# Box layout by VectorE block transposes and four channel picks per image, instead of small matmuls, in a four-layer convolution kernel on one Trainium2 core

## What is computed

```python
h = jnp.einsum('oc,bchw->bohw', w1, x)          # 64 -> 16 channels
h = jax.nn.relu(_bn_train(h, g1, b1))
h = _box_conv(h, x_min, x_max, y_min, y_max)    # 16 -> 64: four boxes for each channel
h = _bn_train(h, g2, b2)
return jax.nn.relu(x + h)
```

## Time and profile before

| what | value |
|---|---|
| runs | 166.64, 165.84, 166.61 us (median 166.61) |
| profiled execution | 165.47 us, of which the span in the trace is 163.7 us |
| PE busy | 147.1 us, 90% |
| DVE, ACT, POOL busy | 110.9, 89.7, 56.9 us |
| L3, by the trace | from about 135 us to 163.7 us |
| granted PE clock, mean | 0.982 of full speed |

### The profile page before, as it was taken

How to read it: one execution, slowest core, us unless ns; L and a number is a source line. 1 busy time by engine, 2 the same in 40 slices (tenths; PEclk the granted TensorE clock), 3 DMA queues, 4 the chain that set the end, 5 groups by cost and what they waited for, 6 DMA issues and landing times.

```text
span 163.7 us, 2908 instructions
## 1 busy us (share of the span) xinstructions
PE 147.1 (90%) x1094; PEld 72.5 (44%) x1094; DVE 110.9 (68%) x264; ACT 89.7 (55%) x147; POOL 56.9 (35%) x107
## 2 busy tenths in 40 slices
PE   7988999999999999999999997999699999999500
PEld 2253432323232422322347754784277647899300
DVE  2386599997699997999815454688860776515880
ACT  3346375757558876568706008992662433672480
POOL 6018999999999700000004000000190000000270
PEclk9999999999999999999999999999999999999975
DMA  3694000000000000000000000000000000000007
GB/s 97 130 326 195 4 0 2 0 2 0 0 6 0 0 0 0 0 4 0 0 0 0 0 2 4 0 0 0 0 0 4 0 0 4 4 4 2 0 6 252
DMA packets 1886, 4.29 MB, mean 26 GB/s; under 512 B 208, under 2 KB 592, under 8 KB 1744
## 3 DMA queue, kind: packets, MB, share of 16 engines
q1 hardware_dynamic: 1728, 3.98, 7.5%
q10 hardware_dynamic: 144, 0.13, 0.3%
HBM read 3.06 MB, written 1.05 MB: 25 GB/s over the span
## 4 chain that ended last, share of the span: by engine, by line
PE 65%; DVE 16%; issue 8%; ACT 5%; DMA 2%; ACTq 0%; DVEq 0%
PE ps L405 13%; PE ps L375 12%; PE ps L364 11%; PE ps L418 11%; DVE nmax L924 5%; PE ps L519 3%; DVE dz L832 3%; PE ps L570 2%; DMA wbc<-wa 2%; ACT box_t L616 2%; PE ps L460 2%; PE ps L338 2%; PE ps L327 2%; PE ps L579 2%; PE ps L421 1%
## 5 line engine op out<-in xcount | busy, mean ns | idle before, releaser
L616 ACT ACTIVATE probs<-ps,nmax 128x1024 f32<-128x1024 f32 x32 | 35.7, 1115 | 27.2 <-DVE nmax L924 26.7
L924 DVE TENSOR_REDUCE nmax<-ps 128x1 f32<-128x1024 f32 x32 | 39.0, 1220 | 6.5 <-PE ps L364 6.2
L375 PE MATMUL ps<-probs,dz 128*64 128x512 f32 x128 | 32.8, 615 | 1.1 <-DVE dz L832 0.9
L364 PE MATMUL ps<-c,b 64*128 64x512 f32 x128 | 32.0, 613 | 0.5 <-ACT probs L616 0.5
L405 PE MATMUL ps<-img,wq 128*128 128x512 f32 x84 | 23.7, 422 | 2.7 <-ACT img L616 1.7
L405 PEld LDWEIGHTS ps<-img,wq 128*128 128x128 f32 x84 | 14.9, 189 | 12.5 <-issue 5.4
L418 PE MATMUL ps<-img,wq 64*128 64x512 f32 x72 | 19.4, 414 | 0.2
L421 PE MATMUL ps<-img,wq 64*128 64x512 f32 x72 | 19.5, 415 | 0.0
L364 PEld LDWEIGHTS ps<-c,b 64*128 64x128 f32 x128 | 11.0, 186 | 18.3 <-issue 9.3
L375 PEld LDWEIGHTS ps<-probs,dz 128*64 128x64 f32 x128 | 6.5, 135 | 24.6 <-DVE dz L832 12.4
L839 DVE TENSOR_TENSOR img<-y,img 128x512 fp32r<-128x512 f32 x12 | 8.9, 739 | 9.8 <-ACT y L616 9.8
(11 more groups left out here) (152 smaller groups left out, 201.9 us busy)
## 6 DMA issues: line engine op xcount, KB each, us to landing
wraw<-wconv SPq DMA_DIRECT2D x1, 1152.0 KB, 8.8
xd<-x SPq DMA_DIRECT2D x4, 256.0 KB, 5.5
out<-box_t SPq DMA_DIRECT2D x4, 256.0 KB, 2.8
consts<-cst SPq DMA_DIRECT2D x1, 327.0 KB, 5.8
wdd<-wa SPq DMA_DIRECT2D x1, 192.0 KB, 2.4
parm<-par SPq DMA_DIRECT2D x1, 163.0 KB, 2.4
wbc<-wa ACTq DMA_DIRECT2D x1, 131.0 KB, 3.8
```

What stands on the lines that cost most here:

```text
L364: last = mm(o[:, 512 * p:512 * p + 512], b32[across, b % 2, j], c32[across, b % 2, :], start=True, stop=True)
L375: last = mm(y[64 * p:64 * p + 64, :], dz[:, g % 4, :], probs[:, g % 3, 512 * p:512 * p + 512], start=False, stop=t == JT - 1)
L616: return nc.scalar.activation(o, i, f, **kw)
L924: V.tensor_reduce(nmax[:, i:i + 1], slot(("S", i)), AX.X, ALU.min).then_inc(max_ready, 1)
```

## The change

Both tensors now reach the box layout with VectorE's transpose of 32x32 blocks (which works within each group of 32 partitions).

- The residual: `spread(b)` uses the selection as weights (128 x 32) and streams the whole image, 512 columns, once for each box. Four matmuls of 512 columns replace 64 of 32. ACT copies the result with the factor 1/15 into y2 (free since L1), reordered to (column, row), and VectorE transposes y2 into xf, 128x512 for each image. In xf the 16 channels now lie next to each other, so one channel is read with a step of 16 elements (64 bytes).
- h: VectorE transposes each half of hs (128x256) straight into hblk, which shrinks to [128, 16, 32]. There are no transposing matmuls, no copies from PSUM, and no zeroes to write.
- `box_rows(g)`: for each channel four matmuls of 32 x 32 weights and 128 columns, each on partitions 32k to 32k+31 for input and output (the diagonal 32x32 tiles of the array), all four into the same PSUM bank. 64 matmuls in place of 16.
- `spread(2)` stands between the two parts of the bottleneck, `spread(3)` and three keep_busy ahead of the statistics matmul, eleven keep_busy behind it.
- Constants: the column tables and the image mask follow the plain partition order; their shapes stay. The loops of L0 to L2 are the same.

```diff
@@ box layout buffers
-        hblk = sb("hblk", [OC, 128])
+        hblk = sb("hblk", [OC, H])
-        xf, fo, ts = (box_t[:, i, :].rearrange("q (o n) -> q o n", o=OC) for i in range(3))
+        fo, ts = (box_t[:, i, :].rearrange("q (o n) -> q o n", o=OC) for i in (1, 2))
+        xf = box_t[:, 0, :].rearrange("q (n p o) -> q n p o", p=2, o=OC)
+        def pairs(t):
+            return t.rearrange("q (n p) -> q n p", p=2)
@@ TensorE
-            def residual(b, s):
-                col = xi[:, b, :].rearrange("q (r s) -> q r s", s=S2)[:, :, s]
-                pick = ident_bf[:].rearrange("q (p o x) -> q p o x", p=2, x=BOX)
-                for x_ in range(BOX):
-                    last = mm(ps[32 * x_:32 * x_ + 32, BANKS[1][b], 32 * s:32 * s + 32], col, pick[:, :, :, x_],
-                              start=True, stop=True)
-                return last
-            def residuals(b, h):
+            def spread(b):
                 pe.wait_ge(xi_ready, b + 1)
-                for s in range(8 * h, 8 * h + 8):
-                    last = residual(b, s)
+                pick = ident_bf[:].rearrange("q (p o x) -> q p o x", p=2, x=BOX)
+                for x_ in range(BOX):
+                    last = mm(ps[32 * x_:32 * x_ + 32, BANKS[1][b], :], pick[:, :, :, x_], xi[:, b, :],
+                              start=True, stop=True)
                 last.then_inc(xt_ready, 1)
-            residuals(0, 0)
-            residuals(0, 1)
+            spread(0)
+            spread(1)
             bottleneck(0, 1, 2)
+            spread(2)
             bottleneck(3).then_inc(h_raw, 1)
-            residuals(1, 0)
-            keep_busy(2, BANKS[0][3])
+            spread(3)
+            keep_busy(3, BANKS[0][3])
             pe.wait_ge(h_stat, 1)
             mm(ps[:, AVG_BANK, 0:48], consts[:, K_SUM8:K_SUM8 + 128], h_parts[:].rearrange("q i n -> q (i n)"),
                start=True, stop=True).then_inc(h_all, 1)
-            residuals(1, 1)
-            keep_busy(2, BANKS[0][3])
-            residuals(2, 0)
-            keep_busy(1, BANKS[0][3])
-            for sq in range(4):
...
-            residuals(2, 1)
-            residuals(3, 0)
-            residuals(3, 1)
-            pe.wait_ge(hblk_act, 4)
-            pe.wait_ge(hblk_dve, 4)
+            keep_busy(11, BANKS[0][3])
+            pe.wait_ge(hblk_ready, 2)
             def box_rows(g):
-                pe.wait_ge(xf_ready, g + 1)
+                pe.wait_ge(xs_ready, g + 1)
                 for o in range(4 * g, 4 * g + 4):
-                    last = mm(ps[:, BANKS[1][g], 128 * (o % 4):128 * (o % 4) + 128], hblk[:, o, :], rows_w[:, o, :],
-                              start=True, stop=True)
+                    for k in range(4):
+                        q = slice(32 * k, 32 * k + 32)
+                        last = mm(ps[q, BANKS[1][g], 128 * (o % 4):128 * (o % 4) + 128], hblk[q, o, :], rows_w[q, o, :],
+                                  start=True, stop=True)
                 last.then_inc(t_ready, 1)
@@ ScalarE
             def x_out(b):
-                act.wait_ge(xt_ready, 2 * (b + 1))
-                run(xf[:, :, 32 * b:32 * b + 32], ps[:, BANKS[1][b], :].rearrange("q (j o) -> q o j", o=OC), ACT.Copy,
-                    scale=1.0 / LEVELS).then_inc(xf_ready, 1)
+                act.wait_ge(xt_ready, b + 1)
+                run(y2[:, b, :].rearrange("q (s r) -> q s r", r=H),
+                    ps[:, BANKS[1][b], :].rearrange("q (r s) -> q s r", s=S2), ACT.Copy, scale=1.0 / LEVELS)\
+                    .then_inc(xs_ready, 1)
-            act.wait_ge(rows_ready, PIECES)
-            x_out(0)
+            for b in range(NB):
+                x_out(b)
...
-            for half in range(2):
-                act.wait_ge(tr_ready, half + 1)
-                for q in range(2):
-                    block_copy(q, half, lambda o, i: run(o, i, ACT.Copy)).then_inc(hblk_act, 1)
-            x_out(1)
             rows_out(0)
-            x_out(2)
             rows_out(1)
-            x_out(3)
             rows_out(2)
             rows_out(3)
@@ VectorE
             for half in range(2):
-                dve.wait_ge(tr_ready, half + 1)
-                for q in range(2, 4):
-                    block_copy(q, half, V.tensor_copy).then_inc(hblk_dve, 1)
+                dve.wait_ge(h_ready, half + 1)
+                V.transpose(hblk[:].rearrange("q o m -> q m o")[:, 16 * half:16 * half + 16, :],
+                            hs[:, 256 * half:256 * half + 256]).then_inc(hblk_ready, 1)
+            dve.wait_ge(rows_ready, PIECES)
+            for b in range(NB):
+                dve.wait_ge(xs_ready, b + 1)
+                V.transpose(box_t[:, 0, HALF * b:HALF * b + HALF], y2[:, b, :]).then_inc(xf_ready, 1)
             def final_sum(o):
-                V.scalar_tensor_tensor(fo[:, o, :], box(o), f_a[:, o:o + 1], xf[:, o, :], ALU.mult, ALU.add)\
-                    .then_inc(f_add, 1)
+                V.scalar_tensor_tensor(pairs(fo[:, o, :]), pairs(box(o)), f_a[:, o:o + 1], xf[:, :, :, o],
+                                       ALU.mult, ALU.add).then_inc(f_add, 1)
@@ GpSimd
-            pool.wait_ge(pv_done, NB * JT)
-            G.memset(hblk[:], 0.0).then_inc(hblk_zero, 1)
...
-                G.tensor_tensor(fo[:, o, :], fo[:, o, :], xf[:, o, :], ALU.add).then_inc(f_sum, 1)
+                G.tensor_tensor(pairs(fo[:, o, :]), pairs(fo[:, o, :]), xf[:, :, :, o], ALU.add).then_inc(f_sum, 1)
```

More of the change, by code:

```diff
@@ L61 @@
 D_AFTER = 3
-H_BANK, HT_BANK, AVG_BANK = 6, 4, 5
-HT_BANKS = (4, 5)
+H_BANK, AVG_BANK = 6, 5
 F_BANKS = (6, 6, 4, 4, 5, 2, 0, 7)
@@ L205, in build @@
         y_of = (y1, y2, y3)
[L207 to L211, removed]
         def image(part, b, kh=1, ds=0, q=slice(0, 128)):
@@ L237, in build @@
         wq_ready = sems("wq_ready", 4)
-        wq_zero, borders_zero, hblk_zero = (sem(n) for n in ("wq_zero", "borders_zero", "hblk_zero"))
+        wq_zero, borders_zero = sem("wq_zero"), sem("borders_zero")
         tanh_done, wmax_part, wmax_done = sem("tanh_done"), sem("wmax_part"), sem("wmax_done")
@@ L249, in build @@
             "h_raw", "h_stat", "h_all", "h_var", "h_sqrt", "h_ab", "h_ready"))
-        tr_ready, hblk_act, hblk_dve = sem("tr_ready"), sem("hblk_act"), sem("hblk_dve")
+        hblk_ready = sem("hblk_ready")
         t_ready, ts_act, f_ready = sem("t_ready"), sem("ts_act"), sem("f_ready")
-        xt_ready, xf_ready = sem("xt_ready"), sem("xf_ready")
+        xt_ready, xs_ready, xf_ready = sem("xt_ready"), sem("xs_ready"), sem("xf_ready")
         f_stat, f_avg, f_dev_done, f_sqr, f_vavg, f_var, f_sqrt, f_bias, f_scale, f_add = (sem(n) for n in (
@@ L546, in _ @@
                start=True, stop=True).then_inc(h_all, 1)
-            residuals(1, 1)
-            keep_busy(2, BANKS[0][3])
-            residuals(2, 0)
-            keep_busy(1, BANKS[0][3])
-            for sq in range(4):
-                if sq % 2 == 0:
-                    pe.wait_ge(h_ready, sq // 2 + 1)
-                cols = slice(128 * sq, 128 * sq + 128)
-                last = mm(ps[:, HT_BANKS[sq // 2], cols], hs[:, cols], consts[:, K_ID:K_ID + 128], start=True, stop=True)
-                if sq % 2:
-                    last.then_inc(tr_ready, 1)
-            residuals(2, 1)
-            residuals(3, 0)
-            residuals(3, 1)
-            pe.wait_ge(hblk_act, 4)
-            pe.wait_ge(hblk_dve, 4)
+            keep_busy(11, BANKS[0][3])
+            pe.wait_ge(hblk_ready, 2)
             pe.wait_ge(rows_ready, PIECES)
@@ L734, in _ @@
                     ACT.Relu, bias=h_b[:], scale=h_a[:]).then_inc(h_ready, 1)
-            act.wait_ge(hblk_zero, 1)
-            for half in range(2):
-                act.wait_ge(tr_ready, half + 1)
-                for q in range(2):
-                    block_copy(q, half, lambda o, i: run(o, i, ACT.Copy)).then_inc(hblk_act, 1)
-            x_out(1)
+            act.wait_ge(cols_placed, NB)
             rows_out(0)
-            x_out(2)
             rows_out(1)
-            x_out(3)
             rows_out(2)
@@ L1205, in _ @@
             pool.wait_ge(wmax_done, 1)
-            pool.wait_ge(pv_done, NB * JT)
-            G.memset(hblk[:], 0.0).then_inc(hblk_zero, 1)
-            pool.wait_ge(hblk_zero, 1)
             pool.wait_ge(ev_ready, 1)
@@ L1238, in constants @@
     r = q % 32
-    w = 8 * (q // 8 % 4) + 2 * (q // 32) + q % 2
     k[:, K_IR:K_IR + 32] = n - r[:, None]
     k[:, K_IR1:K_IR1 + 32] = n - r[:, None] + 1
-    k[:, K_JW:K_JW + 32] = n - w[:, None]
-    k[:, K_JW1:K_JW1 + 32] = n - w[:, None] + 1
-    k[:, K_MASK:K_MASK + 4] = (q[:, None] // 2 % 4) == np.arange(4)
+    k[:, K_JW:K_JW + 32] = n - r[:, None]
+    k[:, K_JW1:K_JW1 + 32] = n - r[:, None] + 1
+    k[:, K_MASK:K_MASK + 4] = q[:, None] // 32 == np.arange(4)
     k[:, K_PART:K_PART + 8] = q[:, None] // 16 == np.arange(8)
```

1 line of the change is left out of this document (removed).

## The result

The median of the changed kernel is 164.94 us over 20 runs, that of the kernel before 166.51 us over 20. The ratio is 0.9904, with a 95% interval of 0.9886 to 0.9923: 1.6 us less (1.3 to 1.9). The prediction was 165.1 us, 1.5 us less. The profiled execution took 164.68 us with a span of 162.7 us; before it was 165.47 and 163.7.

The account below looks back on a forecast made before the run. It took two equally long covers ahead of the box rows, then GpSimd's finish plus 5.05 us, as the bound; 0.2 - 1.83 - 0.15 + 0.3 = -1.5 us from 166.61 gave 165.1 us, range 164.2 to 167.4.

Parts of the forecast that it names:

- Two covers of the same length: Before the box rows, residual matmuls and VectorE's h copies end together; removing only one would give nothing.
- spread(2) delays h by 0.2 us: Between the bottleneck parts, spread(2) holds image 3's column group, so everything behind on h's chain comes 0.2 us later.
- Transposes of h, 0.43 us: Two 128x256 VectorE transposes into hblk at 0.43 us each (bounds 0.27 and 0.70); box rows 1.83 us earlier without spread(2)'s delay.
- Box rows as fast as box columns: 32 matmuls a group on diagonal tiles; two groups take 1.9 us, so -0.15 us ahead of columns 0.
- Transposes of the residual, 0.70 us and hidden: Four 128x512 VectorE transposes, 2.8 us in all, end before the box statistics with 0.2 us of cover; no cost.
- Rows 3 worth nothing: The last box-row group saves as much as the others, but waits stand around it, so it counts 0.
- GpSimd's strided reads, 0.3 us: At the end, GpSimd's sums read xf with a 64-byte step: 0.08 us more each, four times on the path, +0.3 us.
- VectorE's strided reads, 0: VectorE's late sums with the same step cost 0; a doubled slope, 0.3 us behind the fourth issue, kept for the range.
- The end, GpSimd's finish plus a fixed 5.05 us: The span's end hangs on GpSimd finishing its four channels, then the first output issue, plus a fixed 5.05 us.
- The clock, no cost: PE idles twice, some 0.5 and 0.6 us; the granted clock was expected to stay up, so no cost.
- three rivals: VectorE's transposes become the bound (0.15, 167.4 us); diagonal tiles take turns (0.08, 176); strided reads eat half (0.12, 165.7).

Follow-up runs that it names:

- e1: The changed kernel with the residual back on the old 256 TensorE matmuls, only h moved the new way; ratio to the kernel before 0.9977.
- e2: The kernel before with the new way for the residual alone, h kept the old way; ratio to the kernel before 1.0001.
- e5: The changed kernel with the residual's transposes writing xf with channels contiguous, so the sums read plainly; ratio to the kernel before 0.9941.
- e3: The changed kernel with the two box-row loops exchanged, so one diagonal tile's four matmuls follow each other; ratio to the kernel before 1.0619.
- e8: As e6, with the four output pieces sent in the order in which they are finished; ratio to the kernel before 0.9831.
- e4: The changed kernel without the eleven keep_busy matmuls behind the statistics of h; ratio to the kernel before 1.0060.
- e7: The changed kernel with each of the residual's four VectorE transposes done twice; ratio to the kernel before 1.0023.
- e6: As e5, with the fourth residual transpose moved behind the deviations of the first eight channels; ratio to the kernel before 0.9897.

## Why the prediction was right

The size, the sign, the place and the path to the end were right; some terms of the sum were not.

1. *Two covers of the same length.* Right, and shown by e1 and e2.
2. *spread(2) delays h by 0.2 us.* Wrong, it was 0: the statistics of h start at 2.59 in L3 in both kernels. The last instruction that makes xi of image 3 ends at 136.69 before and at 137.02 now, 1.68 and 1.67 us in L3, and image 3's bottleneck starts right behind it (137.08), with spread(2) already issued. The alternative stood in the text; I took the other.
3. *Transposes of h, 0.43 us.* They take 0.607 us, nearer to the upper bound of 0.70, and e5 shows on the residual that a write step makes a transpose slow; for h, which writes with a step of 128 bytes, this was not tried by itself. The copy of 256 elements that I took as the nearest row writes 16 neighbouring elements at a time, and so does not price the step. The box rows came 1.71 us earlier, where I had 1.63, since this error and that of step 2 cancel.
4. *Box rows as fast as box columns.* Right: 1.88 us for two groups, -0.10 for -0.15. The rule on one PSUM bank (the Trainium skill, TensorEngine Tiling (Array Packing), Restrictions and Gotchas) does not hold for outputs on different partitions. By it the 64 records would have gone one by one, which takes 0.109 us a record on one tile (e3), and they went at 29 ns.
5. *Transposes of the residual, 0.70 us and hidden.* Right: 0.668, and the cover was 0.8 us where I had 0.2, mostly since they follow each other every 0.6 us. Statistics 1.81 us earlier (predicted 1.78).
6. *Rows 3 worth nothing.* Off by 0.24 us: with 32 small matmuls its weight loads start 0.36 us behind those of the means matmul instead of 0.21, and the variance matmul now stands behind it. Of its 0.29 us of delay the timeline puts 0.20 down to issue, and their cause is not shown.
7. *GpSimd's strided reads, 0.3 us.* Right: 0.061 us each, 0.24 in all; the estimate by the ratio of the Trainium skill (GPSIMD Engine Reference, Performance pitfalls for Q7 kernels) was 0.08 each.
8. *VectorE's strided reads, 0.* The cost was 0, but not for the reason given. I leaned on a write row that shows no price, and a sum takes 0.074 us more. The last result came late and held the fourth issue by the 0.3 us of my upper end; it cost nothing because the end hangs on the first issue.
9. *The end, GpSimd's finish plus a fixed 5.05 us.* Right: 5.0 us in ten of eleven traces, with the fourth issue late or not. Only another order of the pieces changed it (e8).
10. *The clock, no cost.* The number was right, the argument was not. I had leaned on a clock that stayed at 1.00 through an idle second. In the changed kernel it fell at 154.0, 0.35 us after the last matmul; e4 shows that 3.2 us without a matmul bring it down for the box rows. What kept it up were the eleven keep_busy.

None of the three rivals came: the transposes have 0.8 us of cover (e7), the diagonal tiles overlap (29 ns a record), and the strided reads cost 0.24 us, not 0.9.

In the measure of the traces: 0 - 1.71 - 0.10 + 0.24 + 0.24 = -1.33, which is what the first issue gained; the same terms predicted were 0.2 - 1.83 - 0.15 + 0 + 0.3 = -1.5. By the runs it is 1.6. That 1.5 is so near to both is in part luck: the 0.2 of step 2, which did not come, made up for most of the 0.24 of step 6, which no term had.

## What to carry to other kernels

Before you take away what the chain of waits shows, look at what else ends at the same moment; here one of two parts alone gave 0.4 us and the other nothing, and only both moved the path. A change of layout must be priced at its last reader, and only where that reader holds the path: the 64-byte step in xf cost nothing where it was made, 0.24 us at GpSimd's sums, and nothing at VectorE's, although they took 0.9 us more. A step in the writes instead, with one transpose put into an engine's gap (e6), cost nothing at all. Before you price a late last result, look at what the end follows: here it was the first transfer, not the last. And where outputs are sent in a fixed order, send them in the order in which they are finished.

## What was not expected of the hardware

- VectorE's transpose of 32x32 fp32 blocks: 668 ns for 128x512 and one every 0.6 us with plain writes; 1054 ns with a write step of 512 bytes; 607 ns for 128x256 with a step of 128 bytes.
- A clock that falls while PE's busy share is 1.00: with at most two of the four diagonal tiles at work (e3) the granted clock fell to 0.50 (1.2 GHz in place of 2.4) at 144.7 us and came back at 151.5, in the box columns.
- After TensorE's last matmul the clock fell within 0.4 us in the changed kernel and 3.0 us after it in the kernel before (the last matmul ended at 154.9, the clock was at 1.00 until 157.9). Idle time alone does not tell when it falls.
- The end of the span follows the first of four back-to-back transfers of 256 KB by 5.0 us, even where the fourth is issued 0.3 us late: the DMA engines move 383 GB/s at a busy share of 1.05 by then.
- TensorE begins matmuls of the next 32x32 tile while three of the eight records of the tile ahead are still to start, by the chains of starts in e3.
